# A fused block of 16-head attention and FP8 feed-forward: the last head's sums of squares of y as products with a column of ones, and four operations of the head loop in another order

## The reference

```python
xn = (x - mean(x)) / sqrt(var(x) + 1e-5)
q, k, v = xn @ Wq, xn @ Wk, xn @ Wv
q, k = rmsnorm(q, q_w), rmsnorm(k, k_w)
scores = q @ k.T / sqrt(D) - slope[h] * max(t - s, 0)     # causal
y = softmax(scores) @ v
y = rmsnorm(y, sub_w)                # y / sqrt(mean(y*y) + 1e-5) * sub_w
out += y @ Wproj[h]
```

## Time and profile before

| | |
|---|---|
| Three runs | 549.4, 550.86 and 550.92 us, median 550.86 |
| Profiled execution | 549.36 us, its span (first to last instruction) 547.6 us |
| Busy share of the span | PE 95%, PEld 85%, DVE 82%, ACT 69%, POOL 63% |
| Chain that ended last, by engine | PE 71%, ACT 12%, DVE 8%, issue 6%, POOL 1%, DMA 1% |
| Mean granted clock of PE | 0.983 of full speed |
| HBM | 9.51 MB read, 1.05 MB written |

### The profile page before, as it was taken

How to read it: one execution, slowest core, us unless ns; L and a number is a source line. 1 busy time by engine, 2 the same in 40 slices (tenths; PEclk the granted TensorE clock), 3 DMA queues, 4 the chain that set the end, 5 groups by cost and what they waited for, 6 DMA issues and landing times.

```text
span 547.6 us, 11939 instructions
## 1 busy us (share of the span) xinstructions
PE 519.7 (95%) x3334; PEld 467.1 (85%) x3334; DVE 450.2 (82%) x1099; ACT 377.5 (69%) x855; POOL 345.7 (63%) x494
## 2 busy tenths in 40 slices
PE   8869899999999999999999999999999999999875
PEld 3859698899989898989989899898988999897764
DVE  5668788988898897988889888979889888988863
ACT  2758577686867868676876868677786868677530
POOL 4659486784858478583858658583867848474311
PEclk9999899999999999999999999999999999999986
DMA  5200101001010100001010100101010000000002
GB/s 149 68 1 2 38 1 40 1 2 40 2 39 0 38 0 29 10 0 38 0 38 0 37 1 0 38 0 38 0 38 0 0 10 0 11 1 1 2 0 78
DMA packets 18615, 10.84 MB, mean 20 GB/s; under 512 B 2208, under 2 KB 18592, under 8 KB 18592
## 3 DMA queue, kind: packets, MB, share of 16 engines
q1 hardware_dynamic: 17600, 10.49, 6.5%
q10 hardware_dynamic: 992, 0.07, 0.1%
HBM read 9.51 MB, written 1.05 MB: 19 GB/s over the span
## 4 chain that ended last, share of the span: by engine, by line
PE 71%; ACT 12%; DVE 8%; issue 6%; POOL 1%; DMA 1%; ACTq 0%; DVEq 0%; SPq 0%; POOLq 0%
PE pT_ps L586 10%; PE qkv_ps L507 8%; PE qkv_ps L509 7%; PE qkv_ps L508 7%; PE yT_ps L507 5%; PE yT_ps L509 5%; PE yT_ps L508 5%; ACT probs L793 4%; PE score_big L507 4%; PE score_big L509 3%; PE score_big L508 3%; DVE pT_lo L960 2%; ACT qT_hi L786 2%; ACT stage L773 2%; ACT pT_hi L801 2%
## 5 line engine op out<-in xcount | busy, mean ns | idle before, releaser
L960 DVE TENSOR_TENSOR pT_lo<-pT_ps,pT_hi 128x384 fp32r<-128x384 f32 (+1 forms) x192 | 100.7, 552 | 28.5 <-ACT pT_hi L801 28.4
L773 ACT ACTIVATE stage<-qkv_ps 128x384 f32<-128x384 f32 x119 | 58.6, 492 | 94.8 <-PE qkv_ps L509 93.4
L793 ACT ACTIVATE probs<-probs,neg_max 128x1024 f32<-128x1024 f32 (+7 forms) x128 | 98.6, 771 | 13.2 <-DVE neg_max L951 12.5
L801 ACT ACTIVATE pT_hi<-pT_ps 128x384 fp32r<-128x384 f32 (+1 forms) x192 | 86.6, 486 | 29.0 <-PE pT_ps L586 26.0
L586 PE MATMUL pT_ps<-ident,probs 128*128 128x128 f32 x576 | 86.8, 278 | 8.1 <-ACT probs L793 4.9
L507 PE MATMUL qkv_ps<-w_hi,xT_hi 128*128 128x384 f32 x242 | 88.4, 365 | 0.7 <-DVE xT_lo L1033 0.7
L586 PEld LDWEIGHTS pT_ps<-ident,probs 128*128 128x128 f32 x576 | 65.9, 141 | 24.1 <-DVE pT_lo L960 8.7
L509 PE MATMUL qkv_ps<-w_hi,xT_lo 128*128 128x384 f32 x242 | 81.6, 337 | 0.0
L508 PE MATMUL qkv_ps<-w_lo,xT_hi 128*128 128x384 f32 x242 | 81.4, 336 | 0.0
L401 POOL TENSOR_TENSOR qk_r<-qk_ms,minus_half 128x4 f32<-128x4 f32 x64 | 65.0, 1015 | 19.3 <-DVE qk_ms L925 17.5
L507 PE MATMUL yT_ps<-pT_hi,v_hi 128*128 128x256 f32 (+1 forms) x224 | 72.7, 325 | 0.4 <-DVE pT_lo L960 0.4
(11 more groups left out here) (193 smaller groups left out, 1355.3 us busy)
## 6 DMA issues: line engine op xcount, KB each, us to landing
w_raw<-in_wq SPq DMA_DIRECT2D x16, 128.0 KB, 2.2
w_raw<-in_wk SPq DMA_DIRECT2D x16, 128.0 KB, 2.3
w_raw<-in_wv SPq DMA_DIRECT2D x16, 128.0 KB, 2.4
wp_raw<-in_wproj SPq DMA_DIRECT2D x16, 128.0 KB, 2.1
acc<-in_x SPq DMA_DIRECT2D x4, 256.0 KB, 5.1
out<-acc SPq DMA_DIRECT2D x8, 128.0 KB, 1.8
w<-in_ffn_w ACTq DMA_DIRECT2D x1, 64.0 KB, 5.9
q_col<-in_q_w ACTq DMA_DIRECT2D x1, 0.5 KB, 3.0
```

Source lines behind the costliest of these rows:

```text
L773: act.activation(stage_of(h, k // 2)[:, k % 2, :], qkv_bank(h, k)[:, 0:3 * D], ACT.Copy).then_inc(qkv_read, 1)
L793: act.activation(probs[:, s % 2, 0:(i + 1) * P], probs[:, s % 2, 0:(i + 1) * P], ACT.Exp, bias=neg_max[:, par, s:s + 1], scale=-1.0, accum ...
L801: act.activation(pT_hi[g][:, a:b, r * P:(r + 1) * P], pT_ps[(CHUNK0[s] + k) % 2][:, 0:(b - a) * P].rearrange("p (j t) -> p j t", t=P), ACT ...
L960: dve.tensor_tensor(pT_lo[g][:, a:b, r * P:(r + 1) * P], pT_ps[(CHUNK0[s] + k) % 2][:, 0:(b - a) * P].rearrange("p (j t) -> p j t", t=P), ...
```

## The change

It has two parts.

1. For the last head alone, part_y, split_y and sum_y are left out. `sum_last_y` takes their place on PE: four products per group, each with a 128 x 128 slice of the squares as weights and a column of ones as the moving operand, which give the sums as one column per row tile. `y_mean` is then one DVE operation. The squares are plain float32, not float32r.
2. In all heads: sum_y of group 0 stands behind projection 1 in step 1 (PE); probs_hi(4) ahead of exps(5), and qk_hi(1) behind both (ACT); y_lo of group 1 ahead of add_out(0, 0) in step 2 (DVE); eps * row_sum^2 is formed on ACT behind y_hi (as a Square with a scale) rather than on DVE. add_ffn waits for add_out(0, 0), since both now follow each other closely on `acc`.

```diff
@@ norm of y, POOL
             over_heads(pool, head)
-            split_y(H - 1, 0)
             norm_y(H - 1, 0)
-            split_y(H - 1, 1)
             norm_y(H - 1, 1)
@@ PE
+            def sum_last_y(g):
+                pe.wait_ge(y_squared, 2 * (H - 1) + g + 1)
+                if g == 0:
+                    pe.wait_ge(misc_read, misc_done(H - 1, "proj1a"))
+                else:
+                    pe.wait_ge(scores_masked, NT * H)
+                for r in range(4):
+                    last = pe.matmul(sum_ps(H - 1, g)[:, r:r + 1], y_sq[:, g, r * P:(r + 1) * P], ones[:, 0:1],
+                                     start=True, stop=True)
+                last.then_inc(y_crossed, 1)
...
                     if s == 1:
-                        if not first:
-                            sum_y(h - 1, 0)
                         if not last and not first:
                             project(h + 1, 1 - par, 1)
                         if not first:
+                            sum_y(h - 1, 0)
                             attend(h - 1, 1 - par, 1, 1)
...
             project_out(H - 1, 1, 0, 0, H)
-            sum_y(H - 1, 0)
+            sum_last_y(0)
...
-            sum_y(H - 1, 1)
+            sum_last_y(1)
@@ ACT
-            def y_hi(h, g):
+            def y_hi(h, par, g):
                 act.activation(yT_hi[:, g, :], yT_ps[:, :], ACT.Copy).then_inc(y_hi_done, 1)
+                past(act, y_meaned, 2 * h + g)
+                act.activation(y_pick[:, :, 8], row_sum[:, par, g, :], ACT.Square,
+                               scale=EPS ** 0.5).then_inc(el2_ready, 1)
...
-                    if s % 2:
+                    if s % 2 and s != 5:
                         exps(h, par, s)
                     if s > 0:
                         probs_hi(h, s - 1)
                     elif not first:
                         probs_hi(h - 1, NT - 1)
+                    if s == 5:
+                        exps(h, par, s)
+                        if not last:
+                            qk_hi(h + 1, 1 - par, 1)
...
-                    if s == 4 and not last:
-                        qk_hi(h + 1, 1 - par, 1)
@@ DVE
             def y_mean(h, par, g):
...
-                dve.scalar_tensor_tensor(y_pick[:, :, 8], row_sum[:, par, g, :], EPS, row_sum[:, par, g, :],
-                                         ALU.mult, ALU.mult).then_inc(el2_ready, 1)
+                if is_last(h):
+                    dve.wait_ge(y_crossed, n + 1)
+                    dve.wait_ge(el2_ready, n + 1)
+                    dve.scalar_tensor_tensor(y_ms[:, g, :], sum_ps(h, g), 1.0 / D, y_pick[:, :, 8],
+                                             ALU.mult, ALU.add).then_inc(y_meaned, 1)
+                    return
...
-                    if s == 2 and not first:
-                        part_y(h - 1, 1)
...
+                    if s == 2 and not first:
+                        part_y(h - 1, 1)
+                        y_lo(h - 1, 1)
                     if s in (2, 3) and not first:
                         add_out(h - 1, 0, s - 2)
...
-                    if s == 2 and not first:
-                        y_lo(h - 1, 1)
...
             add_out(H - 2, 1, 1)
-            part_y(H - 1, 0)
             y_mean(H - 1, 1, 0)
             add_out(H - 1, 0, 0)
             y_lo(H - 1, 1)
-            part_y(H - 1, 1)
             add_out(H - 1, 0, 1)
             y_mean(H - 1, 1, 1)
```

More of the change, by code:

```diff
@@ L118, in build_block @@
         quarters = sb("quarters", [P, P], f32r)
+        ones = sb("ones", [P, 1])
         quarter_row = sb("quarter_row", [P, 32])
@@ L353, in _ @@
             pool.memset(minus_half[:, :], -0.5)
+            pool.memset(ones[:, :], 1.0)
             link(pool.memset(ident[:, :], 0.0))
@@ L525, in bank_free @@
                     pe.wait_ge(y_picked, 2 * h - 1)
-                if job == "qkT1" or tail and bank == "qkv":
-                    past(pe, y_picked, 2 * h - 1 if tail else 2 * h)
+                if job == "qkT1":
+                    past(pe, y_picked, 2 * h)
+                if tail and bank == "qkv":
+                    pe.wait_ge(y_meaned, 2 * h - 1)
                 if same:
@@ L882, in head @@
                     if s == 2 and not first:
-                        y_hi(h - 1, 1)
+                        y_hi(h - 1, 1 - par, 1)
                     if s in (2, 3, 4) and not last:
@@ L898, in head @@
                         square_y(h, 0)
-                        y_hi(h, 0)
+                        y_hi(h, par, 0)
             over_heads(act, head)
@@ L903, in _ @@
             square_y(H - 1, 1)
-            y_hi(H - 1, 1)
+            y_hi(H - 1, 1, 1)
         @block.vector
```

13 lines of the change are left out of this document (5 added, 8 removed).

## The result

| | before | after |
|---|---|---|
| Median of six runs each | 550.87 us (548.08 to 551.16) | 534.82 us (533.58 to 536.04) |
| Ratio, 95% interval | | 0.9722, 0.9696 to 0.9747 |
| Profiled execution, its span | 549.36, 547.6 us | 534.62, 532.6 us |
| Mean granted clock of PE | 0.983 | 0.994 |
| Busy share of the span | PE 95%, PEld 85%, DVE 82%, ACT 69%, POOL 63% | PE 96%, PEld 88%, DVE 82%, ACT 71%, POOL 65% |

The change takes 16.1 us off the median, where 14.7 were forecast (550.86 to 536.2). The last two lines of the table split it in the profiled execution. The joining product of the last head that opens its step 1 (L622 before, L631 after) comes 9.5 us sooner: that is the loop. From there to the end the program is 5.5 us shorter: that is the end. Forecast were 7.1 and 6.8, so the loop gave more than was said and the end less, and the two misses partly cancel in the total.

The account below looks back on a forecast made before the run. PE bounds the loop (62.54 of 63 us busy); at the end it waits and its clock falls. Terms 4.3 + 2.5 + 4.5 + 1.9 + 0.7 = 13.9 us off 549.36 give 535.5, forecast 536.2 us, range 532.5 to 541.5.

Parts of the forecast that it names:

- 4.3 + 2.5 = 6.8 us: Program's end: 4.3 us gained up to the last group's squares, 2.5 us from those squares to the last acc pair.
- The ones products: First half of the end: the four products with the ones column cost 1.1 us, bounds 0 and 1.6.
- rival of dearer products: At the end, float32 products run as four passes each, 2.4 us per four; 2.0 us less gain, 538.2 us; chance 0.26.
- The clock: In y's second group at the end, PE keeps full clock: 3.4 us instead of 5.7, a gain of 2.3.
- the clock stays low: Rival: the ones products do not keep the clock up, the group takes 5.7 us, 2.3 less gain; chance 0.08.
- The second half: After the last squares start: yT_lo at 1.1 us, acc pairs at 1.7, 3.9 and 4.7; gain 2.5 us.
- 15 x 0.30: ACT's reordering of pT_hi, exps(5) and qk_hi(1) ends PE's late probs transposes in heads 0 to 14: 4.5 us.
- 7 x 0.27: Group 0's joining product behind projection 1 no longer waits for y_pair, in seven heads: 1.9 us.
- The term for yT_lo: yT_lo of group 1 ahead of add_out(0, 0) removes PE's 0.19 us FFN wait in eight heads; half taken, 0.7 us.
- "nothing" for ACT's operation of four elements: Moving this operation from DVE to ACT, 32 times, changes no time; at most 6 us cost if ACT's cover were gone.
- The loop's waits only move: Rival: DVE and ACT hold PE up instead, only the end's gain remains, 543.3 us; chance 0.10.
- Slower: Rival: y_crossed comes late for DVE, costing 13 us over 15 heads, 556 us; chance 0.03.

Follow-up runs that it names:

- The repeat: The changed kernel again with no edit, on another chip beside runs of the kernel before: median 533.48 us, ratio 0.9719.
- part 1 alone: The kernel before with only the last head's sums of squares made by products with the column of ones: median 543.54 us, ratio 0.9897.

## Why the prediction was right

**The total** came out at 534.82 us for 536.2 forecast, inside the range (532.5 to 541.5). The repeat, 533.48, lies inside as well. That the total fits this well is in part luck: in the profiled execution the loop gave 2.4 us more than forecast and the end 1.3 less.

**The end: mechanism and sum right.** The forecast gave 4.3 + 2.5 = 6.8 us. The tail is 6.8 us shorter with part 1 alone and 7.1 in the repeat (4.7 in the first half and 2.4 in the second). Single terms:
- *The ones products*, 1.1 us taken, took 0.80, inside the bounds of 0 and 1.6. The Trainium skill (FP8 and Floating Point Precision, TensorE Precision Notes) has four passes for a true FP32 product. This case records two matmuls of some 0.10 us each per product, and one in float32r; whether a record is more than one pass no run shows. The price is 0.80 us, so the measurement decides against the rival of dearer products and its 2.4 us.
- *The clock* stayed up as forecast in the part-1 kernel and the repeat. In the first profiled execution it did not, and the group took 5.1 us, between the forecast's 3.4 and the rival's 5.7. That execution carries 1.6 us of the rival "the clock stays low", to which 0.08 was given. What the forecast put wrongly is the reason: that a gap no longer than the products themselves "should leave the clock up". The same gaps did both. A fall of the clock at the end was also one of the forecast's own signs of being wrong, and in that execution it came.
- *The second half* is right to 0.1 us in each of its four starts.

**The loop: mechanism right, size too small**, 9.5 us for 7.1. The term "15 x 0.30" (0.60 per pair) is the one that was too small: the transposes gained 0.89 per pair. It counted the first late start alone, and not what that start does to the next transposes, nor the late fourth transposes of q and k. "7 x 0.27" (0.27 per pair) measured 0.35, for the same reason. The forecast held that PE runs "8 us and more" without another wait behind each one named. One of its three stretches, 477.3 to 484.8, is only 7.5 us long, and such late starts as that at 371.29 show no idle time in their rows, so they were not seen. The term for yT_lo halved a late start of 0.19 per pair, but 0.18 of it was real. Against this stands the 0.09 lost at the joining product of group 1, which the forecast did not have. The "nothing" for ACT's operation of four elements is right for the operation on ACT (0.21 us each, in the row below, no wait of PE behind it), right for the kernel before, as the kernel with this move alone shows, and right in the sum, since no place of the 1.33 us belongs to it. What it missed is that the other moves lean on it: with the operation back on DVE they lose 0.44 us per pair, about 3 us in all. The four costs of undoing add up to 0.90 + 0.49 + 0.28 + 0.44 = 2.11 us per pair, while all four moves together gained 1.40. So they overlap, and costs of undoing are not shares of a gain. ACT's operation in the view of one source line (ns min/median/max):

```profile
L821 ACT ACTIVATE y_pick<-row_sum x32: 206/213/233, 58.6 to 525.2; 128x4 f32<-128x4 f32 x32
```

**The rivals.** "The loop's waits only move" did not come: the pair is 1.40 us shorter. The view of PE's waits over 100 to 460 us is empty after the change, which says little, since before it has a single wait of 0.2; but the kernel with the square on DVE shows the first wait that would have taken their place. "Slower" did not come, since y_pick on DVE found its operand ready with 0.49 us to spare behind it. One new small wait stands at the last head as well, which the forecast did not have (timeline of PE, the joining product of group 1, behind add_out, which yT_lo now precedes; with that move undone it starts without the wait):

```profile
504.79 0.25 PE L631 MATMUL misc<-y_pair,quarters 128*128 128x32 f32 x1 [0.18 <-DVE acc L1018]
```

## What to carry to other kernels

When an engine is 99% busy, its busy time is a poor measure of what is left. Count its instructions in a stretch, or take the time from start to start of the same instruction one loop later: here the busy time gained 0.45 us in 63 and the loop 1.40. A wait that is removed should be costed by its late start plus what it does to its successors, and an operation that nobody waits for today should be costed again as if the waits ahead were gone, because relief on a side engine can be worth nothing alone and 0.44 us per pair together. To find where a gain comes from, compare two traces product by product, start to start. A chain over three engines for a sum across partitions is worth replacing by thin products where it stands in the open, at the end of a program; in the loop the same chain was covered.

## What was not expected of the hardware

- The same program with the same waits of PE, the longest 1.1 us, had its clock at 0.50 for some 3.4 us at the end in one profiled execution and at 1.00 in the same stretch of another. One profile does not tell what clock a short stretch gets.
- A joining product of 32 columns holds its successor up for 0.03 us when it follows without a wait, and for 0.13 us when it starts late.
- A small DVE operation (128 x 4 elements) that starts while a POOL operation on larger tiles runs (v_lo, w_lo, qk_n or v_hi) ends 0.02 to 0.03 us behind it, and takes up to 1.56 us instead of 0.15: all 19 operations on y_pick over 0.18 us in the trace before, and all 15 of those on qk_ms in the trace with the square on DVE. Beside POOL's y_r (128 x 4 elements) the operation on qk_ms kept its 0.17 us, 13 times in that trace.
